# First eight heads of the softmax probabilities transposed in 32x32 blocks by VectorE and exchanged through DRAM

## The reference, cut to what matters

```python
def attention(q, k, v, mask):
    scores = jnp.einsum('bhqd,bhkd->bhqk', q, k) / jnp.sqrt(jnp.float32(HD))
    scores = scores * mask - 10000.0 * (1.0 - mask)
    probs = jax.nn.softmax(scores, axis=-1)
    return jnp.einsum('bhqk,bhkd->bhqd', probs, v)

# layer 0
x = hidden_states + merge_heads(attention(...qkv of layernorm 1...)) @ w_ao + b_ao          # phase A
x = x + merge_heads(attention(q of layernorm 2, kv of encoder_states, cross_mask)) @ w_co + b_co   # phase B
x = x + gelu(layernorm3(x) @ w1 + b1) @ w2 + b2                                             # MLP
# layer 1
a = layernorm(audio_kv)                                                                     # phase D
Q, K, V = hidden @ Wq.T, a @ Wk.T, a @ Wv.T
scores = jnp.where(mask, scores * scale, -inf)
return hidden + jnp.tanh(gate) * (softmax(scores) @ V) @ Wo.T
```

## Time and profile before

| | us |
|---|---|
| median of three runs | 1138.39 (1138.02 to 1139.32) |
| the profiled execution | 1137.63 |
| its span in the trace | 1136.3 |
| TensorE busy | 1112.6 (98%) |
| VectorE busy | 826.8 (73%) |
| ScalarE busy | 719.5 (63%) |
| GpSimd busy | 459.7 (40%) |
| DMA queue of SP, share of 16 DMA engines | 39.7% |

### The profile page before, as it was taken

How to read it: one execution, slowest core, us unless ns; L and a number is a source line. 1 busy time by engine, 2 the same in 40 slices (tenths; PEclk the granted TensorE clock), 3 DMA queues, 4 the chain that set the end, 5 groups by cost and what they waited for, 6 DMA issues and landing times.

```text
span 1136.3 us, 26121 instructions
## 1 busy us (share of the span) xinstructions
PE 1112.6 (98%) x9701; PEld 996.5 (88%) x9701; DVE 826.8 (73%) x1351; ACT 719.5 (63%) x2450; POOL 459.7 (40%) x337
## 2 busy tenths in 40 slices
PE   7999999999999999999999999999999999999998
PEld 6888988989888898887899999999998889888886
DVE  7667777687877787797866567556657678777777
ACT  4677777767778777786443443434435486677776
POOL 3675566557767766675611112112112432122100
DMA  6444443344445555655131130230328244555422
GB/s 209 116 119 129 125 131 93 105 131 135 131 147 156 148 144 161 164 159 169 41 94 61 34 93 29 65 93 1 93 66 225 71 118 114 133 124 131 114 60 85
DMA packets 226238, 128.36 MB, mean 113 GB/s; under 512 B 169680, under 2 KB 177088, under 8 KB 226112
## 3 DMA queue, kind: packets, MB, share of 16 engines
q1 hardware_dynamic: 226112, 126.69, 39.7%
HBM read 93.75 MB, written 32.89 MB: 111 GB/s over the span
## 4 chain that ended last, share of the span: by engine, by line
PE 78%; DVE 7%; ACT 7%; DMA 3%; issue 2%; POOL 2%; SPq 1%; DVEq 0%; ACTq 0%
PE psum L611 20%; PE psum L758 13%; PE psum L782 13%; PE psum L702 9%; PE psum L605 9%; PE psum L645 6%; PE psum L627 4%; ACT prob L1028 4%; PE psum L678 3%; POOL prob L1775 1%; ACT inputs_transposed L1063 1%; DMA weights_whole<-weights_in 1%; DMA normalised<-ln_tile 1%; DVE context_lo L1467 1%; DVE prob L1380 1%
## 5 line engine op out<-in xcount | busy, mean ns | idle before, releaser
L1028 ACT ACTIVATE prob<-prob,negmax 128x128 f32<-128x128 f32 x768 | 296.8, 394 | 3.7 <-DVE negmax L1393 3.6
L1765 POOL TENSOR_TENSOR inputs_lo<-inputs_transposed,inputs_hi 128x512 fp32r<-128x512 f32 x92 | 126.4, 1395 | 339.5 <-DVE inputs_hi L1353 269.4
L611 PE MATMUL psum<-inputs_hi,weights_hi 128*128 128x256 f32 x768 | 224.6, 293 | 2.9 <-ACT kT L998 0.8
L611 PE MATMUL psum<-inputs_lo,weights_hi 128*128 128x256 f32 x768 | 216.9, 282 | 0.0
L611 PE MATMUL psum<-inputs_hi,weights_lo 128*128 128x256 f32 x768 | 216.9, 282 | 0.0
L1775 POOL TENSOR_TENSOR prob<-prob,mask_bias 128x1024 f32<-128x1024 f32 x64 | 153.0, 2413 | 119.5 <-DVE prob L1380 117.5
L611 PEld LDWEIGHTS psum<-inputs_hi,weights_hi 128*128 128x128 f32 x768 | 146.6, 191 | 7.5 <-issue 1.1
L1028 ACT ACTIVATION_READ_ACCUMULATOR prob<-prob,negmax 128x1 f32 x768 | 149.0, 194 | 0.0
L611 PEld LDWEIGHTS psum<-inputs_lo,weights_hi 128*128 128x128 f32 x768 | 146.9, 191 | 0.2
L611 PEld LDWEIGHTS psum<-inputs_hi,weights_lo 128*128 128x128 f32 x768 | 146.7, 191 | 0.0
L758 PE MATMUL psum<-inputs_hi,weights_hi 128*128 128x256 f32 x512 | 145.2, 284 | 0.8 <-POOL weights_lo L1746 0.8
(11 more groups left out here) (112 smaller groups left out, 2512.7 us busy)
## 6 DMA issues: line engine op xcount, KB each, us to landing
weights_whole<-weights_in SPq DMA_DIRECT2D x72, 256.0 KB, 4.1
normalised<-ln_tile SPq DMA_DIRECT2D x30, 512.0 KB, 2.8
inputs_transposed<-normalised SPq DMA_DIRECT2D x120, 128.0 KB, 3.3
stream<-residual SPq DMA_DIRECT2D x48, 256.0 KB, 2.9
residual<-stream SPq DMA_DIRECT2D x48, 256.0 KB, 3.7
context<-row_sums_spread SPq DMA_DIRECT2D x188, 64.0 KB, 2.0
ln_tile<-stream SPq DMA_DIRECT2D x32, 256.0 KB, 4.3
ln_tile<-x_in SPq DMA_DIRECT2D x16, 256.0 KB, 3.5
```

The source lines that it names most:

```text
L611: mm = pe.matmul(ps[:, bank, GT * part:GT * part + GT], w[:, slot, c, o], a[:, buf, c, :], start=c == 0 and i == 0, stop=c == KC - 1 and i ...
L1028: ins = act.activation(P[:, T * s:T * s + T], P[:, T * s:T * s + T], ACT.Exp, bias=negmax[:, par, s:s + 1], accum_out=total[:, par, s:s + 1])
L1765: pool.tensor_tensor(xlo[:, fill.buf, :, tokens(t)], y, xhi[:, fill.buf, :, tokens(t)].bitcast(f32), ALU.subtract).then_inc(s_rlo if fill. ...
```

## The change

A list `BY_PE` names 16 items (0, 17, 19, 21, 23, 25, 27 to 32, 44 to 47) that stay as they were. For the other 32 of the 48 items (the short description of the change speaks of 31; the list leaves 32: 1 to 16, the even ones from 18 to 26, and 33 to 43):

- VectorE turns the 32x32 blocks of heads 0 to 7 in place, one instruction over 128x1024, at the end of step g (`turn_blocks`), as soon as their exponentials are there.
- SP stores that half of `prob` to a DRAM tensor (`store_blocks`, 512 KB, in step g ahead of `load_transposed`), and in step g+1, between `store_row_sums` and `spread_row_sums`, four gathers bring the blocks back to where a full transpose has them (`bring_blocks`, 128 KB each, rows of 32 floats).
- TensorE transposes only heads 8 to 15, in the place where it transposed heads 0 to 7; the second place is empty. ScalarE copies both PSUM banks in one instruction of 128x1024 (`probs_out`), VectorE copies none.
- `times_v(g)` waits for the one copy and for the four gathers.

```diff
+BY_PE = (0, 17, 19, 21, 23, 25, 27, 28, 29, 30, 31, 32, 44, 45, 46, 47)
...
+            def store_blocks(g):
+                n = moved_number(g)
+                sp.wait_ge(s_turned, n)
+                if n > 1:
+                    sp.wait_ge(s_moved, 64 * (n - 1))
+                sp.dma_start(turned, prob[:, g % 2, 0:NH // 2 * T]).then_inc(s_pst, 16)
+
+            def bring_blocks(g):
+
+                sp.wait_ge(s_pst, 16 * moved_number(g))
+                blocks = turned.rearrange("(i k) (h j q) -> j k h i q", i=4, j=4, q=32)
+                for j in range(4):
+                    dst = prob[32 * j:32 * j + 32, g % 2, 0:NH // 2 * T].rearrange("p (h i q) -> p h i q", i=4, q=32)
+                    sp.dma_start(dst, blocks[j]).then_inc(s_moved, 16)
...
                 if st.prev:
                     store_row_sums(g - 1)
+                if st.prev and g - 1 not in BY_PE:
+                    bring_blocks(g - 1)
+                if st.prev:
                     spread_row_sums(g - 1)
                 if ahead_ln:
                     store_normalised(st.ahead)
                 if st.later and st.later.ln is not None and ahead_ln:
                     load_tiles(st.later)
+                if g not in BY_PE:
+                    store_blocks(g)
                 if st.ahead:
                     load_transposed(st.ahead)
...
             def times_v(g):
-                pe.wait_ge(s_pta, 2 * g + 2)
-                pe.wait_ge(s_ptd, 2 * g + 2)
+                pe.wait_ge(s_pta, copied_by_act(g, 1))
+                if g in BY_PE:
+                    pe.wait_ge(s_ptd, copied_by_dve(g, 1))
+                else:
+                    pe.wait_ge(s_moved, 64 * moved_number(g))
...
                     row_sums(g - 1)
-                    transpose_prob(g - 1, 0)
-                    transpose_prob(g - 1, 1)
+                    if g - 1 in BY_PE:
+                        transpose_prob(g - 1, 0)
+                        transpose_prob(g - 1, 1)
+                    else:
+                        transpose_prob(g - 1, 2)
+                        transpose_prob(g - 1, 3)
                 if not late:
                     if st.prev:
                         row_sums_out(g - 1)
                     project(*st.units[1], U_BANK + 1)
-                if st.prev:
+                if st.prev and g - 1 in BY_PE:
                     transpose_prob(g - 1, 2)
                     transpose_prob(g - 1, 3)
...
+            def probs_out(g):
+
+                act.wait_ge(s_tr, transposed_count(g, 3))
+                act.activation(prob[:, g % 2, NH // 2 * T:].rearrange("p (c n) -> p c n", c=2), ps[:, T_BANK:T_BANK + 2, :],
+                               ACT.Copy).then_inc(s_pta, 1)
...
-                if st.prev:
+                if st.prev and g - 1 in BY_PE:
                     prob_out(g - 1, 0)
+                elif st.prev:
+                    probs_out(g - 1)
...
+            def turn_blocks(g):
+
+                dve.wait_ge(s_exp, 4 * g + 2)
+                P = prob[:, g % 2, 0:NH // 2 * T]
+                dve.transpose(P, P).then_inc(s_turned, 1)
...
                 if st.later and st.later.ln is not None:
                     statistics(st.later)
+                if g not in BY_PE:
+                    turn_blocks(g)
                 if st.ends:
                     stream(g - 2)
```

More of the change, by code:

```diff
@@ L145, with moved_number, transposed_count, copied_by_act @@
         load_over((_u, _c), _c)
+BY_PE = (0, 17, 19, 21, 23, 25, 27, 28, 29, 30, 31, 32, 44, 45, 46, 47)
+def moved_number(g):
+    return g + 1 - sum(k <= g for k in BY_PE)
+def transposed_count(g, c):
+    return sum(4 if k in BY_PE else 2 for k in range(g)) + (c + 1 if g in BY_PE else c - 1)
+def copied_by_act(g, half):
+    return sum(2 if k in BY_PE else 1 for k in range(g)) + (half + 1 if g in BY_PE else 1)
+def copied_by_dve(g, half):
+    return sum(2 for k in range(g) if k in BY_PE) + (half + 1 if g in BY_PE else 0)
 _ORDER = [(A, 0, n) for n in (4, 5, 0, 1, 2, 3)]
@@ L228, in build @@
         normal = nc.dram_tensor("normalised", (2 * GT, H), f32, kind="Internal").ap()
+        turned = nc.dram_tensor("prob_turned", (128, NH // 2 * T), f32, kind="Internal").ap()
         spread = nc.dram_tensor("row_sums_spread", (4, KC * T), f32, kind="Internal").ap()
@@ L246, in build @@
         s_rsp = sem("row_sums_spread")
+        s_pst = sem("prob_blocks_stored")
+        s_moved = sem("prob_blocks_moved")
         s_scores = sem("scores")
@@ L288, in build @@
         s_ptd = sem("probT_by_dve")
+        s_turned = sem("prob_blocks_turned")
         s_clo = sem("ctx_lo")
@@ L633, in transpose_prob @@
                 pe.wait_ge(s_exp, 4 * g + c + 1)
-                if c >= 2:
+                if g in BY_PE and c >= 2:
                     if c % 2 == 0:
-                        pe.wait_ge(s_pta, 2 * g + 1)
+                        pe.wait_ge(s_pta, copied_by_act(g, 0))
                     else:
-                        pe.wait_ge(s_ptd, 2 * g + 1)
+                        pe.wait_ge(s_ptd, copied_by_dve(g, 0))
                 elif g == 0:
@@ L641, in transpose_prob @@
                 else:
-                    pe.wait_ge(s_cx, 2 * (g - 1) + c + 1)
+                    pe.wait_ge(s_cx, 2 * (g - 1) + c % 2 + 1)
                 for j in range(4):
@@ L715, in times_v_last @@
             def times_v_last(half):
-                pe.wait_ge(s_pta, 2 * 47 + half + 1)
-                pe.wait_ge(s_ptd, 2 * 47 + half + 1)
+                pe.wait_ge(s_pta, copied_by_act(47, half))
+                pe.wait_ge(s_ptd, copied_by_dve(47, half))
                 pe.wait_ge(s_cx, 2 * 46 + half + 1)
@@ L1013, in half_out @@
                     v_out(q, n)
+            def probs_out(g):
+                act.wait_ge(s_tr, transposed_count(g, 3))
+                act.activation(prob[:, g % 2, NH // 2 * T:].rearrange("p (c n) -> p c n", c=2), ps[:, T_BANK:T_BANK + 2, :],
+                               ACT.Copy).then_inc(s_pta, 1)
             def prob_out(g, c):
-                act.wait_ge(s_tr, 4 * g + c + 1)
+                act.wait_ge(s_tr, transposed_count(g, c))
                 act.activation(prob[:, g % 2, 512 * c:512 * c + 512], ps[:, S_BANK + c if g == 47 else T_BANK, :],
```

2 lines of the change are left out of this document (1 added, 1 removed).

## The result

| | before | after |
|---|---|---|
| median of five runs, us | 1138.31 (1138.02 to 1139.32) | 1148.60 (1145.45 to 1153.06) |
| ratio | | 1.0095, 95% interval 1.0068 to 1.0122 |
| profiled execution, us | 1137.63 | 1148.14 |
| span, us | 1136.3 | 1146.8 |

The changed kernel is 10.3 us slower. The prediction was 1121 us, faster, with a range of 1110 to 1134. It was wrong in sign. The five executions of the changed kernel lie 7.6 us apart, those of the kernel before 1.3.

What follows compares the result with a forecast made beforehand. The prediction took TensorE's stream of matmuls as the limit in all three attention phases. From 1137.6 us it took 27.8 for transposes and added 10.8 of waits: 1120.6, given as 1121 us, range 1110 to 1134 (8 of 10).

Steps and rivals of the forecast that it cites:

- The removal, 27.8 us: TensorE, attention phases: one group of 8 transpose halves dropped per moved item, 32 x 0.87 = 27.8 us gained.
- 0.9 us is left. Cost on the path: none taken: VectorE's inverse before TensorE's row sums: 1.2 us of room shrinks to 0.9, so the block transpose costs nothing.
- Free there: 6 x 0.87 = 5.2 of the 27.8 us come home whole: Phase B: only even items move, their gathers fall in odd steps without a heavy queue, so 5.2 us are gained.
- the softmax chain becomes the limit: Rival: no room at the row sums, 12 steps behind fill steps gain nothing, 10.4 us more, 1131; 0.17 with upper bound.
- TensorE waits between 0 and 1.9 us: Product with V after 12 fill steps of A and D: late block gathers, 0.9 us each taken, 10.8 us in all.
- The worked example: Fill step without tile loads: row sums stored at S+7.3, block gathers issued S+7.7 to S+10.7, S being its start.
- the bound for the steps with tile loads: DMA engines drained 11.4 to 12.8 us into the step, block gathers landing at 14.6 to 16.5, step 14.64 long.
- the 2.3 us: The skill's fit for landing a 128 KB DMA, against 3.3 in the trace; waits would be about zero; set aside.
- the factor of 19: The skill's slowdown for a plain DMA transposing by strides, 26 us of DMA work per item; given no weight.
- The rival "slower": Fill steps: SP waits for VectorE, inputs' gathers land late, 34 us of waits in all, 1144.8 us; chance 0.15.
- Its deciding point: The rival "slower": the kernel gets slower from a mean wait of 27.8 / 12 = 2.3 us per fill step.
- free by a little: Spread of the row sums, behind four gathers: 3 us later, covered by VectorE's idle 2.24 us before the inverse.

Runs made afterwards that it cites:

- x5: The changed kernel with TensorE's transposes of all 32 items gone and nothing in their place, no turn, store or gathers: 1121.75 us, ratio 0.9858.
- x11: As x5, but with phase B's six items back on TensorE, so 26 items of A and D left out: 1120.08 us, ratio 0.9843.
- x8: The changed kernel with six transposes of the identity on TensorE ahead of the wait for the blocks of eleven late items: 1137.14 us, ratio 0.9998.
- x4: The changed kernel without the store and the gathers, VectorE's block transpose kept, all 32 items: 1124.30 us, ratio 0.9879.
- x6: The changed kernel, SP issuing block gathers ahead of weights, mask and row sums, tile loads between row sums' store and spread: 1166.86 us, ratio 1.0256.
- x12: The changed kernel with only 14 items moved, nine of phase A and five of D, none of B: 1128.50 us, ratio 0.9923.
- x3: The changed kernel without the four gathers, block transpose and store kept, all 32 items: 1126.64 us, ratio 0.9897.
- x7: As x6, with only the 26 items of phases A and D moved, none of B: 1160.97 us, ratio 1.0200.

## Why the prediction was wrong

The account: −27.8 (transposes off TensorE) + 11.2 (missing in x5, the second chain for the most part) + 2.5 (turn) + 2.3 (store) + 22.0 (gathers) = +10.2, measured +10.3. That it closes proves nothing, since each term is the difference of two neighbouring runs; what the experiments show is the size of each. Against the forecast, which had −27.8 and +10.8, the miss of 27.6 us is made up, but for 0.4, of 11.2 of room that wasn't there and 16.0 by which the way of the blocks, turn and store included, cost more than the waits in the sum.

- **The removal, 27.8 us: right as TensorE's time.** Undisturbed steps of A became 14.36 and 14.66 us long, 0.9 less than in the earlier trace rows; the forecast was 14.4 and 14.64. Busy time fell by 19.0 us only because the mean clock of 0.993 stretches it by some 8 us.
- **VectorE and "0.9 us is left. Cost on the path: none taken": the step that failed first.** With the transposes gone and nothing added, 11.2 us are missing. I measured the room at one place, in A, and took it for the room of every step. In A it held for the most part, as the stretches of x5 show. In late B before the change, the end of the inverse and the start of the row sums lay 0.42, 0.05 and 0.05 us apart (at 463, 479 and 495 us), where I assumed 0.9 after it. "Free there: 6 x 0.87 = 5.2 of the 27.8 us come home whole" was wrong for the same reason (x11). The rival "the softmax chain becomes the limit" had this mechanism; that its 10.4 us are near the 11.2 is luck, since it put them into A and D behind the fill steps and most are missing in B. I gave it a share of 0.17 together with another, as an alternative to the waits, and it came on top of them.
- **"TensorE waits between 0 and 1.9 us": the term that was mis-sized.** The worked example, the step without tile loads, came out as written: in the step from 182.76 the row sums were stored at S+7.1 and the blocks' gathers issued from S+7.5 to S+11.3 (forecast S+7.3, S+7.7 to S+10.7), no wait followed, pitch 14.66. The fault was the bound for the steps with tile loads. I took the drain of the DMA engines there, 10.6 us into the step, and added the store. But the gathers aren't issued until S+10.3 in such a step, because the inputs' gathers start at S+3.8 and the row sums' store at S+9.85 waits behind everything, and the issue itself stretches to 4.62 us. The bound was of the DMA engines, and in such a step the in-order queue came later than they did. Measured were 14 waits, 23.5 us, up to 3.2 each; forecast were 10.8 in 12, at most 1.9 each. The transfers were not the fault: a block gather landed in 3.7 us at the median where the term took 3.3, and neither the 2.3 us nor the factor of 19 that the prediction set aside would have been nearer.
- **The clock: absent from the sum.** No term and no rival had it, though waits up to 1.9 us were in the range. Five falls in the profiled execution stand for some 8 us; the fillers of x8 gave 11.5 back, of which 3 to 5 are the clock by its mean and the rest isn't told apart. All five came with waits beyond the bound of 1.9, but not every such wait brought one. Even with the 11.5 us back the kernel is no faster than before (1137.14), still far from 1121.
- **The rival "slower" had the right sign and another mechanism.** It needed the inputs' gathers late by their landing. Measured, VectorE waited 11.6 us in 12 waits for them against 0.9 before; x4, without any of the new DMAs, has 6.9 in 8, so more than half of that is there without the block store. Its deciding point, a mean wait of 2.3 us per fill step, wasn't reached by the waits alone (23.5 / 12 = 2.0).
- **SP's spread of the row sums, "free by a little": right.** VectorE waited 9.6 us in 11 waits for it, and 10.7 in 9 before the change. In x6, where it is later still, VectorE waits 36.4 us for it and TensorE 37.0 for the inverse behind.
- **Right:** VectorE 823.4 (forecast 823), DMA share 53.4% of the span (0.5; but in D 0.61 where 0.75 was forecast), the one copy of ScalarE (1.0 us against 1.1), landing times under 5 us at the median, the store's small price (2.3 us).

## What to carry to other kernels

Before booking what is taken off the busiest engine, measure the slack of the next chain in every phase and every kind of step, not at one place: the cheap test is to drop the work without replacing it, and here 11.2 of 27.8 us were gone by that alone. For work that goes over an in-order DMA queue, work out the issue time from the fullest step, since in both orders tried here what stood behind four gathers was late; move only the items whose step has a free queue (x12). A wait of TensorE of some 2 to 3 us can cost more than its length, because half the clock for 3 us can follow; a few idle matmuls ahead of the wait made that rarer here, if the wait itself can't be had away.

## What was not expected of the hardware

- TensorE's granted clock was 0.50 for 3 us behind waits of 2.23, 2.33, 2.67, 2.68 and 3.22 us, and the steps behind the last four lost about 1.5 us; behind 1.86 us and less, and behind one of 2.81, it stayed at 1.00. Other runs have it at 0.50 behind a wait of 1.72 us (x3, at 455.2) and at 1.00 behind one of 3.03 (x7, at 1000.6), so no length of a wait decides it. With six transposes ahead of the wait it stayed at 1.00 behind waits of 2.37 and 2.86 us in the profiled execution, and the mean of the median execution rose from 0.994 to 0.997.
- Four gathers of 128 KB took 2.75 us to issue in an emptier stretch of the changed kernel (203.48) and 4.62 us in a full one (98.81); the DMA engines were 0.66 and 0.91 busy meanwhile (a third set, at 190.22, took 3.87 us at 0.90). In these stretches issuing took SP longer where the DMA engines were busier.
- Block gathers of 128 KB in runs of 128 bytes landed in 3.7 us at the median (2.6 to 5.7) with the DMA engines busy 0.6 to 0.7 of the time, little above the 3.3 us of the earlier trace rows.
- VectorE normalised two tiles in 1.50 us in A of the kernel before (178.50) and in 3.62 us where GpSimd's addition of the bias ran beside it (x5, 442.47). That the addition is the reason was not tested apart.
